# First attention's core in groups of four heads with probability sums made apart; last core: both score products at the head of a step

## The reference

```python
def _L0_xattn_ref(x, y, ...):                      # 16 heads of 32
    ...
    ctx = _attn(qT, k.transpose(0, 2, 1, 3), v.transpose(0, 2, 1, 3))              # the first 496 keys
    ctx_dca = _attn(qT, k_dca.transpose(0, 2, 1, 3), v_dca.transpose(0, 2, 1, 3))  # the last 16 keys
    ...
    return (ctx + DCA_WEIGHT * ctx_dca) @ Wo + bo

def _L3_xattn_ref(x, ctx, pos_map, ctx_pos_map, Wq, Wkv, Wout, bout):              # 32 heads of 16, rotated q and k
    ...
    w = jax.nn.softmax(jnp.einsum('bqhd,bkhd->bhqk', q, k) * scale, axis=-1)
    attn = jnp.einsum('bhqk,bkhd->bqhd', w, v)
    ...
```

## Time and profile before

| | us |
|---|---|
| median of 3 runs (3679.55 to 3683.62) | 3682.23 |
| the profiled execution | 3679.52 |
| its span | 3677.7 |
| first core, first M to last add in A | 228.6 to 607.2 |
| last core | 2690.4 to 3136.3 |

### The profile page before, as it was taken

One profiled execution on the slowest core, in us unless ns is written; L12 is line 12 of the kernel. 1 busy time (PEld: TensorE's weight loads), 2 busy tenths in 40 slices (PEclk: granted clock), 3 DMA queues, 4 the chain that ended last, 5 costly groups with the idle time before them and its releaser, 6 DMA issues. The chain is left out here.

```text
span 3677.7 us, 45536 instructions
## 1 busy us (share of the span) xinstructions
PE 2622.3 (71%) x13916; PEld 1204.5 (33%) x13916; DVE 2358.2 (64%) x4171; ACT 1590.1 (43%) x2191; POOL 994.7 (27%) x874
## 2 busy tenths in 40 slices
PE   3978998799564375276667479972978888748991
PEld 1532333344231131021112257751522222324760
DVE  6656664555735535698889766656667777455664
ACT  3534543244221134444444245541646666222870
POOL 5760000000000112476667222215640000001434
PEclk9979999799676586598899689995979999859995
DMA  3542101110000000000000167753531100111995
GB/s 130 206 152 75 58 13 58 38 35 23 3 0 9 19 0 0 1 1 0 0 0 0 46 217 238 238 168 106 227 126 70 51 8 13 76 51 61 331 314 162
DMA packets 148632, 305.96 MB, mean 83 GB/s; under 512 B 18323, under 2 KB 65439, under 8 KB 146038
## 3 DMA queue, kind: packets, MB, share of 16 engines
q1 hardware_dynamic: 125542, 223.49, 17.2%
q0 software_dynamic: 22928, 80.49, 6.7%
HBM read 210.34 MB, written 93.32 MB: 83 GB/s over the span
## 5 line engine op out<-in xcount | busy, mean ns | idle before, releaser
L1970 DVE TENSOR_REDUCE ac_nmax<-ac_M 128x1 f32<-128x512 f32 (+1 forms) x768 | 496.4, 680 | 214.8 <-PE ac_M L1822 213.1
L1951 ACT ACTIVATE ac_PT<-ac_S 128x1024 f32<-128x1024 f32 x384 | 386.1, 1017 | 184.8 <-PE ac_S L1851 182.3
L2700 PE MATMUL sc_y<-sc_hc,ident 128*128 128x512 f32 x512 | 294.1, 659 | 140.9 <-POOL sc_hc L2676 140.5
L2676 POOL TENSOR_TENSOR sc_hc<-sc_h,sc_cs 128x512 f32<-128x512 f32 x256 | 324.2, 1267 | 174.1 <-DVE sc_h L2778 170.2
L2778 DVE TENSOR_TENSOR_SCAN sc_h<-sc_dA,sc_dB 128x512 f32<-128x512 f32 x256 | 309.9, 1212 | 9.7 <-ACT sc_dA L2738 9.7
L1867 PE MATMUL ac_o<-ac_PT,ac_V 128*32 128x512 f32 (+1 forms) x1536 | 276.9, 614 | 1.0 <-ACT ac_PT L1951 0.8
L2738 ACT ACTIVATE sc_dA<-sc_dl,sc_A 128x512 f32<-128x512 f32 x256 | 176.4, 690 | 177.3 <-DVE sc_h L2778 177.3
L2700 PEld LDWEIGHTS sc_y<-sc_hc,ident 128*128 128x128 f32 x512 | 79.6, 193 | 333.5 <-POOL sc_hc L2676 330.4
L2770 DVE TENSOR_TENSOR sc_dB<-ss_du,sc_b 128x512 f32<-128x512 f32 x256 | 168.5, 659 | 15.8 <-PE sc_b L2690 15.8
L1822 PE MATMUL ac_M<-KT,QT 64*128 64x512 f16 (+1 forms) x384 | 133.5, 421 | 41.8 <-DVE ac_nmax L1970 28.6
L813 POOL DMA_INDIRECT mo_g<-normalised,mo_cur x112 | 146.3, 1306 | 61.4 <-POOL mo_cur L809 44.3
(11 more groups left out here) (482 smaller groups left out, 5866.1 us busy)
## 6 DMA issues: line engine op xcount, KB each, us to landing
slot_results<-mo_o SPq DMA_DIRECT2D x56, 512.0 KB, 4.0
mo_up<-in_w_gate SPq DMA_DIRECT2D x24, 704.0 KB, 5.5
mo_up<-in_w_up SPq DMA_DIRECT2D x24, 704.0 KB, 6.9
keys_t<-ap_kto SPq DMA_DIRECT2D x32, 512.0 KB, 2.6
queries_t<-ap_qto SPq DMA_DIRECT2D x32, 512.0 KB, 2.7
mo_up<-in_exp_up SPq DMA_DIRECT2D x32, 512.0 KB, 6.4
mo_dn<-in_exp_down SPq DMA_DIRECT2D x32, 512.0 KB, 7.2
mo_dn<-in_w_down SPq DMA_DIRECT2D x24, 512.0 KB, 7.3
```

What stands on the lines that cost most here:

```text
L1951: nc.scalar.activation(PT[:, n % PTB, :, :], psS[:, 2 * (n % 2):2 * (n % 2) + 2, :], ACT.Exp, scale=SCALE / (SQK * SQK)).then_inc(exp_done, 1)
L1970: last = v.tensor_reduce(out[:, :, 0], sc[:, 0:MAIN], AX.X, ALU.max)
L2676: nc.gpsimd.tensor_tensor(hc[:, m % RC, :], h[:, m % RH, :], cs[:, n % 2, :], ALU.mult).then_inc(hc_done, 1)
L2700: nc.tensor.matmul(py[:, c, :], env.id32[:], hc[:, m % RC, :], start=(n == 0), stop=(n == NS - 1)).then_inc(y_mm, 1)
```

## The change

**First core.** Groups have four heads, so there are 16 groups of 8 units, and PV multiplies two units at once, each head in its own 32 columns of the array (as the last core did already). The values' tile has no column of ones any more. The sums of the probabilities come apart: POOL adds the PT tiles of the first three key tiles (`partial_sums`, L1809 of the new file, four adds of 128x1024 a group), and PE multiplies the sum with a column of ones and the last key tile with the mask (`sums`, eight products a group into the bank `px`). That makes three results to copy and to transpose per group (o, dca, sums) instead of two, for half the number of groups. The last add in A moves from DVE to POOL (`combine`), V is no longer padded, and PT has six slots rather than three. ACT now also waits for POOL's adds before it overwrites a slot.

**Both cores.** The order is by steps of two units: S, S, two M, PV, two M. In the last core the second S stood behind the first two M before. The group's maxima are transposed `LEAD` units ahead of the group: 4 in the first core, 6 in the last one. `AHEAD` follows from that (26 products in the first core, 18 before; 30 in the last one, 38 before).

```diff
-    VC = 1024 // H
-    GH = P // VC
-    NG, NP = H // GH, GH // 2
+    VC, GH, NP = 32, 4, 2
+    NG = H // GH
...
-    PTB = 2 * NP if rope else 3
+    PTB = 4 if rope else 6
...
-    EARLY = 2 if rope else 0
-    AHEAD = 2 * NMG + 2 + 2 * EARLY
+    LEAD = 6 if rope else 4
+    AHEAD = NMG + 2 + 2 * LEAD
...
-        def rows_unit(g):
-            return (g - 1) * UPG - EARLY
+        at_rows = {g * UPG - LEAD: g for g in range(1, TG)}
...
+            def partial_sums(G, kt):
+                for p in range(NP):
+                    n = G * UPG + kt * NP + p
+                    pool.wait_ge(exp_done, n + 1)
+                    if kt == 1:
+                        if G:
+                            pool.wait_ge(sum_mm, G)
+                        first = PT[:, (n - NP) % PTB]
+                    else:
+                        pool.wait_ge(p_added, G * 2 * NP + p + 1)
+                        first = psum3[:, p]
+                    g.tensor_tensor(psum3[:, p], first, PT[:, n % PTB], ALU.add).then_inc(p_added, 1)
...
+                output_weights()
+                for G in range(TG):
...
+                    partial_sums(G, 1)
+                    partial_sums(G, 2)
+                    if G:
+                        combine(G - 1)
...
+            def sums(g):
...
+                pe.wait_ge(d_ev, g + 1)
+                pe.wait_ge(p_added, (g + 1) * 2 * NP)
+                for r in range(GH):
+                    nc.tensor.matmul(px[r * VC:(r + 1) * VC, :], ones[:], psum3[:, r // 2, r % 2, :], start=True, stop=False)
+                for r in range(GH):
+                    n = g * UPG + (TPB - 1) * NP + r // 2
+                    last = nc.tensor.matmul(px[r * VC:(r + 1) * VC, :], which[:], PT[:, n % PTB, r % 2, :], start=False,
+                                            stop=True)
+                last.then_inc(sum_mm, 1)
...
+            for n in range(0, TU, 2):
+                g, s = n // UPG, n % UPG // 2
+                if rope:
+                    scores_t(n + 2)
+                    scores_t(n + 3)
                     more(n)
-                    if n + 3 < TU:
-                        scores_t(n + 3)
                     values(n + 1)
                     more(n + 1)
...
+                else:
+                    scores_t(n + 2)
+                    scores_t(n + 3)
+                    if g and s == 3:
+                        turned(g - 1, 1)
+                    more(n)
+                    values(n + 1)
+                    more(n + 1)
+                if n in at_rows:
+                    maxima_rows(at_rows[n])
...
+                if g and not rope:
+                    if s == 0:
+                        sums(g - 1)
+                    elif s < 3:
+                        turned(g - 1, 2 if s == 1 else 0)
```

More of the change, by code:

```diff
@@ L1731, in _ @@
         def _(sp):
+            whole = a_done if rope else a_sum
             for g in range(TG):
@@ L1817, in scores @@
                 if m % (NG * NMG) == 0 and b:
-                    pe.wait_ge(kq_in[b % 2], 32 * ((b + 1) // 2 if b % 2 else b // 2))
+                    pe.wait_ge(kq_in[b % 2], 32 * loads(b))
                 slot, previous = ring["max", m]
@@ L1823, in scores, with more @@
                                  start=True, stop=True).then_inc(s_done, 1)
+            def more(n):
+                for m in maxima_of(n):
+                    scores(m)
             def maxima_rows(g):
@@ L1924, in _ @@
-            for i in range(NOUT):
-                group_transposes(TG - 1, i)
+                else:
+                    scores_t(n + 2)
[7 more added lines that the diff above has]
+                    maxima_rows(at_rows[n])
+                if g and rope and s == 2:
+                    turned(g - 1, 0)
@@ L1927, in _ @@
+                if g and not rope:
[3 more added lines that the diff above has]
+                        turned(g - 1, 2 if s == 1 else 0)
+            if rope:
+                turned(TG - 1, 0)
+            else:
+                sums(TG - 1)
+                for i in (2, 0, 1):
+                    turned(TG - 1, i)
         @block.scalar
@@ L1940, in group_rows, with slot_free @@
                     act.wait_ge(row_in[g % 2], 16 * NR * (g // 2))
-                bank = pd[:] if rope else psM[:, ring["rows", g][0], :]
+                bank = px[:] if rope else psM[:, ring["rows", g][0], :]
                 nc.scalar.activation(mrow[:, g % 2, :], bank.bitcast(F16)[0:NR, 0:S], ACT.Copy).then_inc(rows_ev, 1)
-            for g in range(TG):
-                if rows_unit(g) < 0:
-                    group_rows(g)
+            def slot_free(n):
+                g, kt, p = of_unit(n)
+                act.wait_ge(pv_done, n - p + NP)
+                if rope:
+                    return
+                if kt == TPB - 1:
+                    act.wait_ge(sum_mm, g + 1)
+                else:
+                    act.wait_ge(p_added, g * 2 * NP + (kt == 2) * NP + p + 1)
+            group_rows(0)
             for n in range(TU):
@@ L2015, in attention_output_block @@
+            if rope:
+                normed(TG - 1, 0)
+            else:
+                inverse(TG - 1)
+                for i in range(2):
+                    normed(TG - 1, i)
 def attention_output_block(nc, env, w):
```

272 lines of the change are left out of this document (150 added, 122 removed).

## The result

| | before | after |
|---|---|---|
| median (4 runs each, on one chip) | 3680.9 us | 3752.4 us (3748.8 to 3755.3) |
| ratio after to before, 95% interval | | 1.0193 (1.0175 to 1.0211) |
| span of the profiled execution | 3677.7 | 3751.7 |
| first core, first M to last add in A | 378.6 | 458.2 |
| last core | 445.9 | 443.5 |

The kernel is 1.9% slower, 71.5 us by the medians. The two cores make 79.6 - 2.4 = 77.2 us, the spans differ by 74.0; the 3 us the other way lie in untouched layers and are assigned to nothing.

The account below looks back on a forecast made before the run. PE's own work was taken to bound the first core, DVE's ring of two banks the last. 3679.5 + 53 (first core) - 5 (last core) = 3727.5, as a median 3730 us; range 3695 to 3775.

Parts of the forecast that it names:

- part 4: First core: S waits for maxima rows right behind their transposes; stall 7.9 and lower clock 1.7, group 25.2 us.
- The stall: First core: S 7.0 us after the maxima's transposes, with eight issues at 0.60 each; PE idles 6.2 us.
- The clock: First core, behind the hole: PE at 1.2 GHz for S, S, T and two M, +1.7 us a group.
- Part 5: First core, POOL: adds of 11.4 us a group hide under the stall; only at the start do they not, +7.
- The wait for POOL's first add: First core's start: the seventh exponential waits for the add, at about 276 instead of 262; +7 us.
- The +4 for groups behind a batch's load: First core: two groups behind a batch's load cost +4 us more.
- End: First core's end: one more T, sums and POOL's add after the last PV, +5; last steps without M, -4.
- part 3: First core's steps without stall: 3.2 us each; with sums and dca product a four-head group takes 15.3 us.
- Rival C: Both cores: rows land before PE asks, so they are no wait; 3570 us, chance 0.03.
- The last core: Step 3.09, group 12.9 instead of 13.28, two groups behind a batch's load +11; sum -5 us.
- A: Longer stall: one us on each of 46 landings, lower clock in the last core; some 3790 us, chance 0.12.
- B: First core: eight issues cost no more than four, clock stays up; 3664 us; decides from 6.4 us stall downwards; chance 0.06.

Follow-up runs that it names:

- experiment 2: Changed kernel with the first core's maxima rows made eight units ahead instead of four (LEAD 8): 3627.5 us, ratio to before 0.9847.
- experiment 1: First core as in the kernel before, last core as changed: 3676.0 us, ratio to before 0.9982.
- experiment 3: Changed kernel with a head's two rows written by one transfer in the first core, four issues a group instead of eight: 3708.8 us, ratio to before 1.0069.
- experiment 4: Changed kernel with 20 extra products on PE ahead of each wait for the rows in the first core: 3721.3 us, ratio to before 1.0096.
- experiment 5: Changed kernel with POOL's four adds a group in the first core cut to 128x16 elements each, sums not right: 3730.9 us, ratio to before 1.0128.
- experiment 6: Changed kernel with POOL preparing the output weights in four pieces between the first core's adds, not before the first: 3747.4 us, ratio to before 1.0173.
- experiment 7: Changed kernel with the scaling of the first core's maxima on ACT instead of DVE: 3735.6 us, ratio to before 1.0150.
- experiment 8: Changed kernel with DVE's scaling of the maxima as a product of two tensors instead of a tensor and a number: 3749.6 us (one run).
- experiment 9: Changed kernel with the rows made eight units ahead in both cores (LEAD 8): 3603.8 us, ratio to before 0.9786.
- experiment 10: Two kernels: LEAD 8 in both cores, one transfer per head, late output weights, 3595.8 us; the same plus scaling on ACT and earlier transposes of o, 3582.2 us.

## Why the prediction was right, and where its sizes were off

**Direction and cause.** Forecast were 3730 us (3695 to 3775); it is 3752. The step that decided, part 4, is confirmed: experiment 2 takes the wait away and 129 us with it, experiment 1 puts the whole loss into the first core.

**The stall (right).** S 7.0 after the transposes and an idle time of 6.2 were forecast; 6.93 and 5.96 came in the group shown, and the idle time is 5.95 to 6.45 in 14 of the 15 groups (18.6 in the first). The price of an issue was right too: eight took 4.84, and experiment 3 gave back what four of them took. The 2.0 us that part 4 sets beside its 1.7, from the Trainium skill, page "DMA: Bandwidth & Descriptors", section "Anatomy of one DMA", are measured there on transfers that GpSimd issues; these are SP's, and from the start of the last of eight issues to S it is 1.6 us here (the issues of 4.84 us end 1.06 before S, each lasting 0.57).

**The clock (mis-sized).** Part 4 let 1.2 GHz last for S, S, T and two M, +1.7. It lasted through PV and part of the dca product, +2.74 by experiment 4 in a group such as the one shown. The earlier trace rows had shown PV at 1.98 behind a shorter hole; the sum should have counted it. That is 1.0 a group.

**POOL (a term that was missing).** Part 5 asked only whether POOL's adds end in time. They do. But DVE's scaling between its reductions is held until the add beside it ends, +1.1 a group (experiments 5 to 8). With these two terms 25.2 becomes 27.3, which is the measured group.

**Start.** The wait for POOL's first add was put at +7; by experiment 6 it is 32.6 - 21.7 = 10.9. The first S was put at 251.5 and came at 250.6. The +4 for groups behind a batch's load did not come: the loads are issued at 369 and 478, and the holes behind them (S at 389.50 and 498.61) are 5.96 like the others.

**End.** From the last group's S (659.69) to the end (686.80) it is 27.1 us; the forecast's terms make 15.3 + 5 - 4 + 3.3 = 19.6. Half the clock holds there too, and the sums and three T behind the last PV form a chain with a wait at each link:

```profile
678.77 1.07 PE L1943 MATMUL ac_x<-ac_psum,ac_ones 128*32 128x512 f32 x8 [1.23 <-ACT ac_oT L2012]
679.62 1.07 PE L1946 MATMUL ac_x<-ac_PT,ac_which 128*32 128x512 f32 x8
681.40 0.66 PE L1963 MATMUL ac_x<-ident,ac_oT 128*128 128x128 f32 x4 [0.71 <-ACT ac_oT L2016]
682.50 0.66 PE L1963 MATMUL ac_x<-ident,ac_oT 128*128 128x128 f32 x4 [0.45 <-DVE ac_rec L2083]
684.01 0.66 PE L1963 MATMUL ac_x<-ident,ac_oT 128*128 128x128 f32 x4 [0.85 <-DVE ac_A L2100]
```

The account of the first core: 15 groups from 250.6 to 659.7 take 409.1, forecast 15 x 25.2 + 7 + 4 = 389, so +20 (not 15 x 2.1, since the early groups and the last are shorter); the end +7.5; the start -0.9. Together 26.6, the difference of 79.6 and 53.

**The steps without a stall (part 3, luck in part).** A group without stall was put at 15.3; without stall it is 17.9 (experiment 2). In the changed kernel the forecast did not suffer from it: T follows S behind the hole without a wait (473.00), and the wait for the bank is in the 1.33 of part 4 (0.72 at 491.68). That the hole covers them was not foreseen. Rival C, priced by that 15.3, would have been wrong: not 3570; experiment 9, in which hardly a row waits, took 3604.

**The last core (right).** Forecast -5, measured -2.4 by the windows, and -4 to -6.5 in the other profiles; a step 3.09, as forecast; a group 12.8 for 12.9; waits for rows of 0.74 to 0.79 in most groups, six longer ones (1.3 to 4.6); the two groups behind a batch's load cost 31.82 - 25.6 = 6.2 and about as much, 12 for 11.

**The rivals.** A needed landings a us later; they came as forecast. B needed eight issues for the price of four and a clock that stays up; neither was so. With four issues in fact (experiment 3) the kernel is still 0.7% slower, in line with its break-even: a group takes 23.9 and two took 21.7.

## What to carry to other kernels

When an edit moves a producer in an in-order schedule, count what lies between it and its consumer before and after, in us, against the whole way of the data (copy, each issue, landing); here two steps of distance were worth 3.5% of the kernel (129 us). A stall's price is not only its hole: count every product behind it at the lower clock until a row shows the clock back. And an engine that is given spare work is not free for its neighbour: look at what that one does in SBUF at the same time.

## What the runs showed of the hardware

- A DVE instruction on 32 numbers a partition that reads and writes SBUF only (0.17 us) is held while POOL adds fp32 tiles in SBUF: 1.47 us, up to the end of the add beside it, though the next add follows at once, and once 8.27 us, behind four in a row. The form (one tensor or two) makes no difference. Not held beside the adds are the reductions out of PSUM (0.67), DVE's product of a PSUM tile and a few numbers in SBUF (0.68 at 447.32 in experiment 2, in adds of 444.60 to 449.28), and ACT on the same SBUF tile (0.22 us). Beside POOL's scaling of a single 128x512 tile DVE's scaling took 0.18 us (at 253.05 in experiment 2, a single reading).
- After an idle time of 3.78 us PE's granted level was 1.2 GHz, and after 5.96 us too. Twenty products in the hole, with 1.64 us idle behind them, kept it at 2.4 GHz in 13 of 15 groups. After about equal holes (5.96 and 5.99 us) the clock was back before PV in one group and behind it in the next (experiment 5), and in experiment 10 S ran at half speed behind a hole of 2.61 us (1.89) in one kernel and at full speed behind one of 2.56 (1.04) in the other. So neither the fall nor the time at the lower level is fixed by the hole alone.
- One transfer of two rows cost SP 0.66 us to issue (2.64 for four), against 0.60 for one row (4.84 for eight), and landed no later: S followed the end of the issues by 1.08 and 1.06 us.
